# Raw expert weights loaded over their own low parts and split in the third batch's max stage, instead of through the probabilities' buffers in the first batch's

## What is computed

```python
x = x + mixer(layernorm(x))          # silu(x @ Win + bin), a decaying scan over the tokens, @ Wout
x = x + cross_attention(layernorm(x), ctx, mask)   # 16 heads of 8, 512 queries, 154 keys, softmax
n = layernorm(x)
gates = sinkhorn((n @ router_w.T + router_b) / temp)          # 3 iterations, 8 experts
topk_vals, topk_idx = top_k(gates, 2)
g, p = relu(einsum('btd,edf->btef', n, wg)), einsum('btd,edf->btef', n, wp)
all_out = einsum('btef,efd->bted', g * p, wo)                 # wg, wp: 8 x 128 x 256
x = n + sum over the two picks of gate * all_out[pick]
```

## Time and profile before

| | us |
|---|---|
| median of 3 runs | 408.7 |
| lowest, highest | 408.17, 410.48 |
| span of the profiled execution, first to last instruction | 417.4 |
| that execution's own time | not given, the span is all there is of it |
| PE busy | 333.2 (80%) |
| DVE busy | 243.6 (58%) |
| ACT busy | 149.9 (36%) |
| POOL busy | 145.7 (35%) |

### The profile page before, as it was taken

The page is one execution under the profiler, slowest core; times in us unless marked ns, Lnnn a source line. Parts: engine busy times, 40 slices in busy tenths (PEclk is TensorE's granted clock), DMA queues, the critical chain, the costliest instruction groups (busy, mean ns, idle before and its releaser), DMA issues.

```text
span 417.4 us, 5742 instructions
## 1 busy us (share of the span) xinstructions
PE 333.2 (80%) x1817; PEld 214.9 (51%) x1829; DVE 243.6 (58%) x672; ACT 149.9 (36%) x298; POOL 145.7 (35%) x179
## 2 busy tenths in 40 slices
PE   1555659679987989888984887567999899799995
PEld 1433436353465544553452542125787777588883
DVE  6585385863397832874359860124545359986662
ACT  2503403806635336105531053322535332223221
POOL 7331222562022140003004058401364375466563
PEclk9985595859999989998999699886899899999998
DMA  4302760431005172062101001241101511242000
GB/s 106 72 1 77 178 196 1 101 67 38 2 0 126 39 152 36 2 142 71 41 2 50 1 25 48 86 127 51 33 22 35 176 63 52 79 151 77 25 0 25
DMA packets 31401, 26.86 MB, mean 64 GB/s; under 512 B 5856, under 2 KB 28066, under 8 KB 31157
## 3 DMA queue, kind: packets, MB, share of 16 engines
q1 hardware_dynamic: 30125, 24.40, 22.7%
q0 software_dynamic: 1248, 2.11, 1.5%
HBM read 19.53 MB, written 7.23 MB: 64 GB/s over the span
## 4 chain that ended last, share of the span: by engine, by line
PE 57%; DVE 22%; issue 7%; ACT 5%; DMA 3%; POOL 3%; SPq 1%; another core or an unknown queue 1%; POOLq 0%; DVEq 0%; ACTq 0%
DVE nmax_mask L1282 5%; PE pC L1711 4%; PE pC L1708 4%; PE pS L1473 3%; PE pS L1476 3%; PE pS L1531 3%; PE pS L327 3%; PE pS L1664 3%; PE pS L328 2%; PE pS L329 2%; PE pS L1667 2%; PE pG L1448 2%; PE pA L329 1%; PE pT L1608 1%; PE pA L327 1%
## 5 line engine op out<-in xcount | busy, mean ns | idle before, releaser
L1282 DVE TENSOR_REDUCE nmax_mask<-pS 128x3 f32<-128x462 f32 (+1 forms) x96 | 52.7, 579 | 19.0 <-PE pS L1667 18.4
L905 ACT ACTIVATE prob<-pS 128x512 f32<-128x512 f32 x80 | 44.0, 597 | 31.2 <-PE pS L1476 15.0
L1664 PE MATMUL pS<-k_stack,q_stack 72*128 72x154 bf16 x256 | 36.5, 249 | 3.3 <-DMA q_stack<-q_scr 3.2
L1667 PE MATMUL pS<-mbias,ident_bf 128*128 128x462 bf16 (+1 forms) x96 | 36.0, 375 | 0.0
L780 POOL TENSOR_TENSOR xi_lo<-late,xi_hi 128x512 fp32r<-128x512 f32 x22 | 28.6, 1300 | 20.6 <-ACT xi_hi L965 20.5
L759 POOL DMA_INDIRECT out_scr<-expert_y,meta x23 | 22.7, 985 | 26.8 <-ACT expert_y L954 21.5
L1473 PE MATMUL pS<-q_stack,k_stack 75*128 75x512 bf16 (+1 forms) x64 | 25.3, 396 | 4.9 <-ACT prob L905 3.0
L1303 DVE RECIPROCAL rz<-pG 128x16 f32<-128x16 f32 x16 | 4.1, 256 | 42.0 <-PE pG L1448 34.3
L1664 PEld LDWEIGHTS pS<-k_stack,q_stack 72*128 72x128 bf16 x256 | 21.9, 108 | 11.7 <-issue 5.9
L1661 PE MATMUL pS<-mbiasT,ident_bf 128*128 128x128 bf16 x72 | 17.7, 245 | 12.6 <-DVE nmax_mask L1282 12.6
L965 ACT CAST xi_hi<-late 128x512 fp32r<-128x512 f32 x22 | 13.7, 621 | 36.3 <-DVE late L1338 35.8
(11 more groups left out here) (396 smaller groups left out, 860.8 us busy)
## 6 DMA issues: line engine op xcount, KB each, us to landing
prob<-w_scr SPq DMA_DIRECT2D x16, 256.0 KB
q_stack<-q_scr SPq DMA_DIRECT2D x9, 384.0 KB
q_scr<-q_parts SPq DMA_DIRECT2D x12, 128.0 KB, 2.4
k_stack<-k_scr SPq DMA_DIRECT2D x36, 40.0 KB
sort_scr<-blank SPq DMA_DIRECT2D x5, 258.0 KB, 5.6
q_stack<-sort_scr SPq DMA_DIRECT2D x5, 258.0 KB, 2.7
res<-in_x_dram SPq DMA_DIRECT2D x4, 256.0 KB, 4.7
prob<-in_L_ffn_wg_dram SPq DMA_DIRECT2D x1, 1024.0 KB, 5.5
```

The lines of the kernel that those rows point to most:

```text
L905: act.activation(prob[:, (NSB * b + n) % NBUF, :], score_bank(b, NSA + n)[:, :], ACT.Exp).then_inc(s_exp, 1)
L1282: dve.tensor_reduce(nmax[:, qt, hs[0]:hs[-1] + 1], score_bank(b, n)[:, 0:len(hs) * KEYS].rearrange("p (h k) -> p h k", k=KEYS), AX.X, ALU. ...
L1664: pe.matmul(dst[:, i * KEYS:(i + 1) * KEYS], q_stack[b % 2][0:STACK, h, qt * P:(qt + 1) * P], k_stack[b % 2][0:STACK, h, 0:KEYS], start=(i ...
L1667: pe.matmul(dst[:, 0:len(hs) * KEYS].rearrange("p (h k) -> p h k", k=KEYS), ident_bf[:, :], mbias[:, qt, :].unsqueeze(1).broadcast_to([P, ...
```

## The change

The raw weights get a buffer that covers the same bytes as `wgp_lo`: it is allocated, given back at once, and `wgp_lo` is allocated in its place. The subtraction that makes the low part then runs in place. The two weight loads leave the prologue (only the two loads of x stay there, as `load_x`, and the wait for the first queries goes) and are issued in slot 29 of batch 1. The eight splits go to every third slot of batch 2's max stage. The exponentials no longer wait for the splits.

```diff
-        wgp = [sb("wgp_hi", [P, E, 2, FF], F32R), sb("wgp_lo", [P, E, 2, FF], F32R)]
+        with nc.sbuf_tensor("wgp_raw", [P, E, 2, FF], F32) as wgp_raw:
+            pass
+        wgp_lo = sb("wgp_lo", [P, E, 2, FF], F32R)
+        wgp = [sb("wgp_hi", [P, E, 2, FF], F32R), wgp_lo]
...
-        wgp_raw = prob[:, 0:2 * E * FF // S, :].rearrange("p u n -> p (u n)").rearrange(
-            "p (e w f) -> p e w f", w=2, e=E)
...
-        EXPERTS_AT = [17, 18, 19, 20, 21, 22, 23, 24]
+        LOAD_EXPERTS_AT = 29
+        EXPERTS_AT = [1, 4, 7, 10, 13, 16, 19, 22]
...
-                 + o0[6:] + q0[:4] + kv0[5:] + q0[4:] + [("mask_T", 0, 0)] + m1[1:] + [("load_experts", 0, 0)])
+                 + o0[6:] + q0[:4] + kv0[5:] + q0[4:] + [("mask_T", 0, 0)] + m1[1:] + [("load_x", 0, 0)])
...
-            if b == 0:
+            if b == 1:
+                place([("load_experts", 0, 0)], [LOAD_EXPERTS_AT])
+            if b == 2:
                 place([("split_experts", 0, n) for n in range(EXPERT_STEPS)], EXPERTS_AT)
...
-                if step == "load_experts":
+                if step == "load_x":

                     for i in range(2, NB):
                         sp.dma_start(res[:, i, :, :], x[i].rearrange("(t p) d -> p t d", p=P)).then_inc(s_x[i], 16)
-                    for chunk in s_qfirst:
-                        sp.wait_ge(chunk, 16 * PARTS)
+                elif step == "load_experts":
+
                     sp.dma_start(wgp_raw[:, :, 0, :], wg.rearrange("e d f -> d e f")).then_inc(s_wgp, 16)
                     sp.dma_start(wgp_raw[:, :, 1, :], wp.rearrange("e d f -> d e f")).then_inc(s_wgp, 16)
...
                     before = NSB * b + n - NBUF
                     if before >= 0:
                         act.wait_ge(s_pv, before // 5 + 1)
-                    else:
-                        act.wait_ge(s_wsplit, EXPERT_STEPS)
```

## The result

The changed kernel takes 406.0 us in the median of 15 runs (403.35 to 409.7), the kernel before 409.6 us in 15 runs beside it (407.9 to 411.24). The ratio is 0.9912, 95% interval 0.9886 to 0.9939: 0.88% faster, 3.6 us. The prediction had 3.2 us less and 405.5 us. Its 405.5 started from the 408.7 of three runs; from 409.6 the same 3.2 us give 406.4.

The account below looks back on a forecast made before the run. The prediction took batch 0's max stage as bound by ACT's expert casts and DVE operations waiting for POOL, up to PE's transposes. Its terms, -3.44 + 0.11 + 0.1 = -3.2 us, took 408.7 to 405.5 us, range 402.2 to 409.0.

Parts of the forecast that it names:

- (a) ACT's casts: Batch 0: without two casts ahead of it, `ctx_hi` starts at 76.17 instead of 76.86, a gain of 0.69 us.
- (b) POOL beside `max_split`: Batch 0: without POOL's expert subtractions, the four small DVE operations of `max_split` end at 82.95 against 86.52 us.
- (c) PE takes over as the last: Batch 0: PE's mask product, 0.43 us, now precedes the transposes of the maxima, at 83.12 instead of 86.56: -3.44 us.
- (d) The dropped waits: Batch 0: the exponentials' wait for the low parts and SP's wait bind nothing, so dropping them gives 0.
- Batch 1's loads: Two weight loads issued near 151 land at about 162, 4 us ahead of the first cast: 0, bound +2 us.
- Batch 2: Max stage receiving the splits: `act_hi` slips by 0.11 us behind a cast, POOL's subtractions cost `max_split` 0.1.
- The clock: TensorE clock in batch 0: nothing gained at the same lag; 1.7 us if it rises 3.4 us earlier against the work.
- The sum: Whole kernel: -3.44 + 0.11 + 0.1 = -3.2 us, from 408.7 to 405.5 us.
- the first: Rival, batch 0: the clock does not fall at all, -3.3 us more, 402.2 us; chance 0.14.
- The second: Rival, batch 2: POOL's subtractions meet `q_split` and `max_split`, price up to 5.7 us, 411.2 us; chance 0.09.
- The third: Rival: the weight loads land late and ACT holds `copy_group` back by up to 2 us, 407.5 us; chance 0.11.
- the fourth: Rival, after batch 0: a low-clock stretch of 3.4 us appears or grows elsewhere, costing 1.7 us, 407.2 us; chance 0.16.

Follow-up runs that it names:

- Experiment 1: Changed kernel with the weight loads back in the prologue and ACT's eight casts back in batch 0, subtractions left in batch 2: 405.34 us, ratio 0.9894.
- Experiment 3: Changed kernel plus eight dummy POOL subtractions that nobody reads, in slots 17 to 24 of batch 0: 412.13 us in a single run.
- experiment 2: Changed kernel with loads in the prologue and the whole splits at their old slots of batch 0, new buffer kept: 409.09 us, ratio 1.0003.
- experiment 4: Changed kernel plus eight POOL memsets of 128x1024, which only write, in slots 17 to 24 of batch 0: 408.12 us in a single run.
- experiment 6: Changed kernel plus seven PE products that nobody reads, in slots 22 and 23 of batch 0: 402.52 us, ratio 0.9849; run again, 402.19 us, 0.9822.
- experiment 8: Changed kernel with its two weight loads and the wait for the first queries back in the prologue, splits left in batch 2: 405.26 us, ratio 0.9891.
- experiment 5: Changed kernel with the eight splits late in batch 2, in slots 17 to 24 instead of 1 to 22: 411.03 us, ratio 1.0034.

## Why the prediction was right

- **(a) ACT's casts, -0.69.** What comes ahead of `max_split` moved by 0.61, since `ctx_hi` started 0.09 us behind PE's transposes (76.50 - 76.41) and not 0.02. Experiment 1 finds 1.09 us for the casts in all, since they also hold back POOL's subtractions for the mixer, which then meet `max_split`. The prediction counted that piece under (b); the sum is not touched by it.
- **(b) POOL beside `max_split`.** Predicted 1.36 us for the four, measured 83.18 - 81.92 = 1.26. Experiment 3 brings 2.70 us back by POOL work alone, experiment 2 all of it, with ACT's casts. The mechanism is shown. It needed one correction, from experiment 4: whether a DVE operation waits depends on its kind and on POOL's. "Waits until POOL's running instruction is done" was too broad, and right for all four here because POOL subtracts.
- **(c) PE takes over as the last.** It does, by 0.40 us. In experiment 6, with PE at full clock, PE is ready first and waits 0.85 us for DVE, and the transposes start 0.34 us earlier by position. The mask product holds it 0.56 us instead of 0.43, and the sum for the stage comes to -3.23 instead of -3.44.
- **(d) The dropped waits, 0.** That of the exponentials: experiment 2, 1.0003. That of SP: experiment 8 has it again and is no slower.
- **Batch 1's loads, 0.** 3.0 us to spare where 4 were forecast, since the load took 12.0 us and not 9.0. Experiment 8 finds no cost in the timed runs.
- **Batch 2, +0.21.** Measured +0.08: `act_hi` slips, and the subtractions miss the exposed operations.
- **The clock.** "At the same lag nothing is gained" is what these two traces show, 6.5 us both times, but the reason behind it does not hold, and this term was right by luck. The lag is 5.1 us in experiment 1 and 5.8 in experiment 2, and in the new trace PE worked without a break from 80.78, 9.3 us before the rise. What sets the moment of the rise stays open. The gain is still there later: the first unit of batch 3 is 3.45 us earlier by position.
- **The sum.** The two stages measure -3.23 + 0.08 = -3.15 in the profile, predicted -3.2; the position at batch 3 has -3.45, and the timed runs have -3.6 us, with an interval from 2.5 to 4.7 us (409.6 times 0.0061 and 0.0114). What may lie between 3.15 and 3.6 is within it, and within what experiment 2's positions differ from those of the kernel before.

Of the rivals, the first was priced well (3.3 us, 3.23 in experiment 6) and didn't occur: 0.61 us less of idle time (1.04 instead of 1.65 us ahead of the fall) kept the clock no higher. Something small would have sufficed, seven products. The second was priced at 411.2 and experiment 5, which provokes it, took 411.0 us, but partly by chance: that price had up to 2.4 us for `q_split`, which the experiment's late slots don't touch, and nothing for the clock, which in the profiled execution cost 4.0 us on top of the 2.91 us of waits (6.9 - 2.91). So 2.91 us of waits already used up the whole gain, less than the 3.2 at which the prediction has the sign turn. That the subtractions just miss `max_split` was worth more than it looked. The third did not come about (experiment 8), and of the fourth, a low stretch elsewhere, nothing is left at batch 3, where the gain is no less than behind batch 0.

## What to carry to other kernels

A small operation that takes several times its usual time in one stage and not in another is a question to the engines beside it: lay the timelines of DVE and POOL over each other before looking for a dependency. Work that is off the critical path on its own engine isn't free; give it a stage in which the engine that it holds up has nothing exposed, and let it end before that stage's last small operations. And a wait on PE is to be priced with the granted clock behind it: here seven products that nobody reads, put into the gaps of one stage, were worth as much (405.97 to 402.19 us) as moving eight casts and eight subtractions.

## What the runs showed that was not expected

- A memset on POOL holds up DVE's casts (1.25 and 0.82 us for one of 0.20) and not its two-input subtraction (0.22 us). The prediction had no such difference.
- A stall of 2.91 us on PE grew to 6.9 us by the next batch, at a granted clock of 0.50 to 0.51 from 185 to 201 us (experiment 5).
- In traces whose batch 0 has the same steps the clock fell at 79.6 or at 82.1 and was low for 13.5 or 10.2 us (the kernel before and experiment 2).
- Two loads of 1 MB ahead of them in the queue made the issue of five fills take SP 10.89 us; six fills without such loads took 4.48, and 4.53 in experiment 8, where the loads are back in the prologue.
